# The last 64 columns of a shared expert's gate and up products, made by one pair of 128-column products in one PSUM bank

## The reference

```python
# x_flat: tokens x 256; shared_gate_w, shared_up_w: 704 x 256; shared_down_w: 256 x 704
shared = jax.nn.silu(x_flat @ shared_gate_w.T) * (x_flat @ shared_up_w.T) @ shared_down_w.T
shared_weight = jax.nn.sigmoid(x_flat @ shared_expert_gate_w.T)
out = out + shared_weight * shared      # out: the sum over the routed experts
```

```python
h = exp(delta * A[:, s]) * h + (delta * u) * B[s];   y += C[s] * h
```

## Time and profile before

| what | value |
|---|---|
| median of 3 runs | 3368.06 us (3366.18 to 3368.32) |
| the profiled execution's own time | 3364.8 us |
| its span, first to last instruction | 3362.8 us |
| mean granted TensorE clock | 0.928 of 2.4 GHz |
| busy: PE, DVE, ACT, POOL | 2834.9, 2546.5, 2064.1, 2592.0 us |

### The profile page before, as it was taken

One profiled execution on the slowest core, in us unless ns is written; L12 is line 12 of the kernel. 1 busy time (PEld: TensorE's weight loads), 2 busy tenths in 40 slices (PEclk: granted clock), 3 DMA queues, 4 the chain that ended last, 5 costly groups with the idle time before them and its releaser, 6 DMA issues. The chain is left out here.

```text
span 3362.8 us, 46770 instructions
## 1 busy us (share of the span) xinstructions
PE 2834.9 (84%) x12696; PEld 1870.1 (56%) x12697; DVE 2546.5 (76%) x4108; ACT 2064.1 (61%) x3786; POOL 2592.0 (77%) x2474
## 2 busy tenths in 40 slices
PE   3686979797979797888888888888887779999998
PEld 2444555555555555555555555565545447777776
DVE  3498989899989989898999898989897842222222
ACT  3576677676767676766767676767665514444443
POOL 1399898989889898989898989898999913444444
PEclk7897989898989898989999999999998889999999
DMA  2001111111111111111110101010112313333333
GB/s 75 23 32 32 36 44 36 43 39 39 39 39 41 38 39 40 46 33 46 34 51 26 51 29 51 29 48 31 43 36 82 101 56 58 63 63 63 62 62 52
DMA packets 113898, 155.37 MB, mean 46 GB/s; under 512 B 15472, under 2 KB 73264, under 8 KB 113712
## 3 DMA queue, kind: packets, MB, share of 16 engines
q1 hardware_dynamic: 77344, 109.32, 10.4%
q0 software_dynamic: 25728, 34.75, 6.4%
q10 hardware_dynamic: 10640, 9.09, 0.8%
HBM read 107.36 MB, written 45.76 MB: 46 GB/s over the span
## 5 line engine op out<-in xcount | busy, mean ns | idle before, releaser
L872 POOL TENSOR_TENSOR dbu<-du,bbc 128x512 f32<-128x512 f32 x1024 | 1294.2, 1279 | 74.5 <-DVE h L1440 67.8
L1440 DVE TENSOR_TENSOR_SCAN h<-bank,dbu 128x512 f32<-128x512 f32 x1024 | 1227.3, 1212 | 158.7 <-ACT bank L1082 101.9
L1082 ACT ACTIVATE bank<-region,amat 128x512 f32<-128x512 f32 x1024 | 703.6, 691 | 313.3 <-DVE h L1440 299.0
L665 PE MATMUL bank<-ident,h 128*128 128x128 f32 x4096 | 624.9, 289 | 259.5 <-DVE acc L1430 231.4
L665 PEld LDWEIGHTS bank<-ident,h 128*128 128x128 f32 x4096 | 495.6, 148 | 544.3 <-DVE acc L1430 224.7
L858 POOL TENSOR_TENSOR acc<-acc,hTc 128x512 f32<-128x512 f32 x480 | 609.6, 1271 | 103.7 <-ACT hTc L1066 102.1
L1607 POOL DMA_INDIRECT out<-ye,ids x136 | 213.3, 1569 | 347.1 <-DMA out<-ye,ids 311.3
L1066 ACT ACTIVATE hTc<-bank,cT 128x512 f32<-128x512 f32 x480 | 327.3, 682 | 236.6 <-PE bank L665 236.5
L1430 DVE SCALAR_TENSOR_TENSOR acc<-bank,cT,acc 128x512 f32<-128x512 f32 x544 | 395.0, 730 | 38.9 <-PE bank L665 33.4
L619 PE MATMUL bank<-x4T,w_su 128*128 128x512 f32 (+1 forms) x768 | 389.2, 610 | 10.7 <-DVE score L1305 10.7
L1643 DVE SCALAR_TENSOR_TENSOR gg<-gt,bank 128x352 f32<-128x352 f32 x136 | 70.7, 520 | 382.2 <-ACT gt L1577 382.2
(11 more groups left out here) (204 smaller groups left out, 4361.1 us busy)
## 6 DMA issues: line engine op xcount, KB each, us to landing
bbc<-b_scratch SPq DMA_DIRECT2D x256, 256.0 KB, 3.1
xe<-slots_in SPq DMA_DIRECT2D x136, 129.0 KB
region<-in_x SPq DMA_DIRECT2D x16, 512.0 KB, 3.8
out<-x ACTq DMA_DIRECT2D x16, 512.0 KB, 3.1
region<-in_e_gu SPq DMA_DIRECT2D x8, 704.0 KB, 5.4
out<-ye,ids POOLq DMA_INDIRECT x136
slots_in<-dbu SPq DMA_DIRECT2D x16, 129.0 KB, 3.2
slots_in<-x,pos POOLq DMA_INDIRECT x128
```

The lines of the kernel that those rows point to most:

```text
L665: last = tr(scan[f"hT{s}.{t}"][:, m * P:(m + 1) * P], h[:, s % 2, m, t * P:(t + 1) * P], ident[:, :])
L872: g.tensor_tensor(dbu[:, n % 4, :], du[:, m, :], bbc[:, (b * NS + s) % NROW, :], ALU.mult).then_inc(S("dbu_ready"), 1)
L1082: f(db(n)[:, :], delta[:, 1 - par, m, :], ACT.Exp, scale=amat[:, m, s:s + 1]).then_inc(S("da_ready"), 1)
L1440: v.tensor_tensor_scan(h[:, s % 2, m, :], db(n)[:, :], dbu[:, n % 4, :], 0.0, ALU.mult, ALU.add)\
```

## The change

For pieces 0 to 4 nothing is computed otherwise. For piece 5 the 64 gate columns and the 64 up columns lie side by side at the end of `w_su` (from column 2 x 640), and one pair of 128-column products fills one bank: rows 0 to 63 hold the gate, rows 64 to 127 the up product. There is no `u5` fill any more; DVE's `up_of(5)` reads the upper half of `g5`'s bank, which stays taken until `su_ready`. The loads of `w_su` become four DMAs.

```diff
+FULL = SI // P * P
@@ in layers, the ring's tiles
         for n in range(len(SC)):
-            late.add(f"g{n}", 1, AT["gate"][n], ("sgate_ready", n))
-            late.add(f"u{n}", 1, AT["up"][n], ("su_ready", n))
+            if n < len(SC) - 1:
+                late.add(f"g{n}", 1, AT["gate"][n], ("sgate_ready", n))
+                late.add(f"u{n}", 1, AT["up"][n], ("su_ready", n))
+            else:
+                late.add(f"g{n}", 1, AT["up"][n], ("su_ready", n))
@@ PE, hidden_of
                     at, size = SC[n]
+                    if n == len(SC) - 1 and half == 1:
+                        return
                     late.may_fill(pe, f"{name}{n}", b, done)
...
-                        last = mm(late[f"{name}{n}", b][0:size, :], w_su[:, c, half * SI + at:half * SI + at + size], x4T[:, c, :],
+                        first, rows = (half * FULL + at, size) if n < len(SC) - 1 else (2 * FULL, 2 * size)
+                        last = mm(late[f"{name}{n}", b][0:rows, :], w_su[:, c, first:first + rows], x4T[:, c, :],
@@ SP, the loads
-                sp_.dma_start(w_su[:, :, half * SI:(half + 1) * SI], a[name].rearrange("(c p) n -> p c n", p=P)).then_inc(w_sloaded, 16)
+                columns = a[name].rearrange("(c p) n -> p c n", p=P)
+                sp_.dma_start(w_su[:, :, half * FULL:(half + 1) * FULL], columns[:, :, 0:FULL]).then_inc(w_sloaded, 16)
+                sp_.dma_start(w_su[:, :, 2 * FULL + half * (SI - FULL):2 * FULL + (half + 1) * (SI - FULL)], columns[:, :, FULL:SI])\
+                    .then_inc(w_sloaded, 16)
@@ DVE, up_of
-                    late.filled(dve, f"u{n}", b)
                     done(dve, "sgate_ready", b, n)
-                    v.tensor_tensor(shh[0:size, n, :], late[f"u{n}", b][0:size, :], shh[0:size, n, :], ALU.mult).then_inc(S("su_ready"), 1)
+                    if n == len(SC) - 1:
+                        up = late[f"g{n}", b][size:2 * size, :]
+                    else:
+                        late.filled(dve, f"u{n}", b)
+                        up = late[f"u{n}", b][0:size, :]
+                    v.tensor_tensor(shh[0:size, n, :], up, shh[0:size, n, :], ALU.mult).then_inc(S("su_ready"), 1)
```

More of the change, by code:

```diff
@@ L612, in hidden_of @@
                     at, size = SC[n]
+                    if n == len(SC) - 1 and half == 1:
+                        return
                     late.may_fill(pe, f"{name}{n}", b, done)
                     if b == 0 and n == 0 and half == 0:
-                        pe.wait_ge(w_sloaded, 16 * (2 + len(SC)))
+                        pe.wait_ge(w_sloaded, 16 * (4 + len(SC)))
                     for c in range(DC):
```

## The result

The changed kernel takes 3483.48 us (median of 6 runs, 3482.36 to 3484.37), the kernel before 3368.43 us in the same rounds (6 runs): the ratio is 1.034, interval [1.033, 1.035], 115 us slower. The profiled execution took 3482.82 us with a span of 3481.1 us and a mean granted clock of 0.903, against 0.928 before.

The account below looks back on a forecast made before the run. A tight chain over DVE, ACT and POOL, with slack on PE, was taken to bound the turn. 13 full turns at 5.4 + 1.8 = 7.2 us, plus 5 and 2, gave 100.6 us more: 3468 us, range 3432 to 3498.

Parts of the forecast that it names:

- The period: Time from one turn's `up_of(5)` to the next: 162.04 us before, forecast to become 169 us.
- `d0` ahead of `hT12.3`: Unit 54: transposes queue behind `d0`'s wait and 12 products, delaying DVE's scan and ACT: 5.4 us a turn, bounds 4 to 6.7.
- The clock: PE's longer pauses before `d0` and the L494 transposes bring half clock: 1.8 us a turn for both, bounds 0 and 5.
- In front of `d0`: PE's pause grows to 3.7 us; half clock costs 1.5 us in two turns of three, taken as 1.0.
- Behind L494: PE's pause before these transposes grows to 6.4 us; half clock in every turn, 0.8 us, bounds 0.5 and 3.
- turn 14: ACT's `hTc` is pushed there too, ahead of a scan that already waited 3.65 us: 5 us.
- turn 15: Two DVE scans of 1.22 us each come behind an addition's existing 4.26 us wait: 2 us.
- The removed products and the wide `g5`: Dropping `u5` saves PE 2.0 us a turn but only lengthens its pause; `g5` at 128 columns: both costed at nothing.
- Partition 64, banks, loads: `up_of(5)` reading partition 64 may lose an overlap, 3 us outside the sum; swapped banks and extra loads costed at nothing.
- Rival 1: The move of `d0` alone costs, with no more half clock: 77 us, 3445 us; chance 0.15.
- Rivals 2, 3 and 5: Half clock to turn's end, 3505 us, chance 0.10; delay partly hidden, 3405, 0.08; saved products cancel early `d0`, within 0.2%, 0.02.
- rival 4: PE sets the turn, so each turn gives back `u5`'s 2.0 us: faster, 3336 us; chance 0.03.

Follow-up runs that it names:

- e1_d0_back: Changed kernel with only `d0` put back to unit 55, behind `hT12.3`, the merged product kept: 3388.0 us.
- e2_move_only: Kernel before the change with `u5` begun one slot earlier, which puts `d0` in unit 54 ahead of `hT12.3`: 3478.6 us.
- e3_fill_d0_pause: Changed kernel with three extra 512-token products in PE's pause before `d0`, overwritten by `d0`: 3440.0 us.
- e13_more_dve: e8_back_filled with one extra DVE copy of 64 partitions x 512 elements a turn, ahead of `gate_of(1)`: 3383.7 us.
- e11_wide_g5_alone: Kernel before the change with the two `g5` products widened from 64 to 128 columns, `u5` kept: 3385.9 us.
- e8_back_filled: e1_d0_back with two extra 512-token products in `d0`'s bank, ahead of the wait for `su_ready`: 3379.3 us.
- e9_lower_half: e8_back_filled with `up_of(5)` reading the lower 64 partitions of its bank instead of the upper ones: 3380.1 us.
- e5_back_up54: e1_d0_back with `up_of(5)` in slot 54 instead of 56, no extra products: 3371.9 us.
- e12_up54_filled: e5_back_up54 with nine extra 256-column products behind `d1`'s first half, in PE's pause before the 16-bit transposes: 3386.9 us.
- e10_thick_g5: e8_back_filled with two extra 512-token products a turn in `g5`'s bank, ahead of its first product: 3388.5 us.

## Why the prediction was right

3468 us with 3432 to 3498 was forecast, and 3483.5 measured. The chain was right. That the sum came so near is in part luck: a full turn was put at 7.2 us more and has 8.0 more, out of a move that was put too high by 0.8 and a clock that was put too low by 1.6. The period was taken from one turn, 162.04 us, which is the shortest of three that alternate; their mean is 162.69, and so 170.67 stands against a forecast of 169. By its own steps:

- **`d0` ahead of `hT12.3`.** Right in place and mechanism, shown from both sides: undone alone it takes 95 us back (`e1_d0_back`), done alone it costs 111 (`e2_move_only`). In size, the scan was to come about 7.4 us behind `up_of(5)` with `d0` at full clock and came at 7.51 (`e3_fill_d0_pause`). In the period this was worth 4.6 us a turn (167.25 less 162.69), not 5.4, though above the lower bound of 4.
- **The clock.** That it falls in both places was right, and both terms were wrong. In front of `d0` I took 1.0 us a turn; `d0` lost 2.2, in every turn and not in two of three, and the period lost 3.4 (170.67 less 167.26). Behind L494 I took 0.8; filling that pause left the held period and the time as they were. The wait grew as forecast (2.67 us of the scan for PE), but the slack behind it took all of it. The two terms came to 1.8, measured 3.4. This is what put the result above the forecast. I had also ordered the cases by the length of the pause, with one of 2.00 us that has no fall; in `e13_more_dve` the clock falls at one of 1.86. The sum was 100.6 us and the spans differ by 118.3: the 13 full turns brought 103.6 instead of 93.6 (95.7 and the 7.9 of the step to turn 14), turn 14 brought 9.0 instead of 5, turn 15 with all that follows 4.7 instead of 2, the start 0.9. In turn 14 `d0` took 10.43 us and the scan stood 11.97 us behind `up_of(5)`; I had left the clock out there.
- **The removed products and the wide `g5`, costed at nothing.** This step failed, by little. A 128-column product isn't priced like a 64-column one here but 0.34 us lower, and the merged form with `d0` back costs 20 us, not 0. On top of the move it is worth only 5 us (3483.5 against 3478.6). Between the profiled executions, 23 us apart, 11.2 lie in the 12 turns, held 1.1 us above the mean of before, and a wide `g5` alone does as much (`e11_wide_g5_alone`, 11.3); 4.6 lie in the step to turn 14; 7.9 lie behind the last turn and go with two products in the pause (`e8_back_filled`). A size, then, that was put at nothing and is 11 to 20 us.
- **Partition 64, banks, loads.** The first is 0.1 us in the row and nothing in the time (`e9_lower_half`). The banks weren't varied by themselves.
- **Rivals.** Rival 1 (the move alone) is what the two runs with a filled pause show, 3440 against its 3445: the clock's fall in `d0` is what kept it from being the result. Rivals 2, 3 and 5 are excluded by the period; rival 4 by `e11_wide_g5_alone` as well. The lower end of the range took 4.5 us a turn, though the move's own lower bound was 4.

One thing in the table helps with the sizes: the held periods stand equally far apart, 163.83, 167.26 and 170.67, that is 3.43 and 3.41 us. Against the merged form with `d0` back (`e1_d0_back`), the move with `d0` at full clock is one such step and the clock's fall in `d0` a second. A delay of 2.2 us in `d0` cost a whole step, and one of 0.7 us on DVE none. So a price read from one pair of kernels (4.6, 3.4, the 1.1 of the merged form) holds for that pair, and they don't add up.

Still open: what makes the steps equal, why eight kernels with different work share a period of 163.8 us while the kernel before and `e5_back_up54` alternate below it, and so which edit would free one of the eight. No version here beats the kernel before.

## What to carry to other kernels

Deleting work from an in-order queue moves what stands behind it: here a saving of 2 us a turn pulled a wait, and 12 products with it, in front of four transposes for which two other engines wait. Ask first what the deletion promotes, and past whom; then whether the operand that it waits for can be made earlier (`up_of(5)` two slots up took back 93 of 115 us). And where an engine has slack, less work on it isn't safe either: 0.7 us less on PE in a turn made this kernel 17.6 us slower (`e11_wide_g5_alone`). More work isn't a cure by rule: products in a pause gave 43 us in one place (`e3_fill_d0_pause`), nothing in a second, and cost 15 us in a third (`e12_up54_filled`).

## What the hardware showed that I had not expected

- **Periods that don't follow the work.** Fourteen kernels show one alternating period near 162.7 us and held ones of 163.83, 167.26 and 170.67, each repeated to some hundredths turn after turn. 0.54 us less on the path (`e2_move_only` against the changed kernel), 0.7 us more on DVE (`e13_more_dve`), or 0.9 us more on PE (`e10_thick_g5`) don't move them. What does move them moves them by 3.4 us at once. In `e13_more_dve` the clock falls at other places of the turn than in `e8_back_filled`, and the sum is the same. That the places of the falls hold the period is an argument from this; no run could switch the clock's changes off.
- **A product of 64 columns costs more than one of 128** when it stands among those of 128: 0.34 us with its neighbours, at full clock. The load itself is shorter, 136 ns a record on average against 194 for the wide ones of the same line before. But neither the narrow load nor the wide one behind it starts ahead of its product, as the loads among wide products do. The page "TensorE: Matmul & The Clock Gate" of the Trainium skill, section "LDWEIGHTS (loading the stationary operand)", has a load's time grow with its columns; the load records agree, and the rows of the products show that the kernel pays the other way round.
